# A graph network's edge stage: eight VectorE instructions of 128 elements per step become two of 512

## The reference, cut to what matters

```python
def _layer(x, ea, src, dst, nw, ew, fnw, fnb, few, feb):
    h = relu(x @ nw.T)
    e = relu(ea @ ew.T)
    e2 = concatenate([h[src] + h[dst], e], axis=-1)
    agg = segment_sum(e, dst, num_segments=x.shape[0])
    n2 = concatenate([agg, h], axis=-1)
    n2 = relu(n2 @ fnw.T + fnb)
    e2 = relu(e2 @ few.T + feb)
    return n2, e2
```

## Time and profile before

| | us |
|---|---|
| three runs | 3683.78, 3673.3, 3674.27 |
| median | 3674.27 |
| the profiled execution's own time | 3683.78 |
| its span | 3682.0 |
| busy: TensorE, VectorE, ScalarE, GpSimd | 3343.9, 2011.2, 1169.9, 2618.3 |
| edge-layers stage, first to last gather started | 2552.46 to 3634.35 |
| the last L2305 starts | 3662.0 |
| 200 us of the stage (3000 to 3200), busy: TensorE, VectorE, ScalarE, GpSimd | 187.19, 171.27, 119.34, 153.35 |

### The profile page before, as it was taken

The page is one execution under the profiler, slowest core; times in us unless marked ns, Lnnn a source line. Parts: engine busy times, 40 slices in busy tenths (PEclk is TensorE's granted clock), DMA queues, the critical chain, the costliest instruction groups (busy, mean ns, idle before and its releaser), DMA issues. The chain is left out here.

```text
span 3682.0 us, 74575 instructions
## 1 busy us (share of the span) xinstructions
PE 3343.9 (91%) x22631; PEld 2291.8 (62%) x22631; DVE 2011.2 (55%) x5296; ACT 1169.9 (32%) x2569; POOL 2618.3 (71%) x2750
## 2 busy tenths in 40 slices
PE   2899994999998899999879999986999999999997
PEld 0566662656666565666646566666777777777775
DVE  7675551232324723232661323275788888888887
ACT  1442220000002600000440000055555655556555
POOL 3777776777775677777467777748777777777773
PEclk6899997999999899999989999998999999999998
DMA  7686554777774777777377777746666666666663
GB/s 288 208 262 194 185 183 151 243 237 239 246 241 145 255 243 245 245 244 244 121 263 243 245 243 245 243 133 177 171 166 168 164 165 165 166 167 164 166 166 82
DMA packets 367699, 747.55 MB, mean 203 GB/s; under 512 B 102785, under 2 KB 197659, under 8 KB 366722
## 3 DMA queue, kind: packets, MB, share of 16 engines
q0 software_dynamic: 134912, 331.04, 31.7%
q1 hardware_dynamic: 224679, 362.01, 30.3%
q10 hardware_dynamic: 7899, 51.90, 3.6%
HBM read 613.65 MB, written 131.02 MB: 202 GB/s over the span
## 5 line engine op out<-in xcount | busy, mean ns | idle before, releaser
L601 POOL DMA_INDIRECT ring<-split_table,src_idx x1240 | 1182.1, 953 | 417.3 <-issue 370.8
L1486 PE MATMUL ps<-spare,acc 128*128 128x500 fp8e4 x5292 | 1158.8, 377 | 97.4 <-DMA spare<-adjacency 67.0
L2124 POOL DMA_INDIRECT ring<-h_table,idx_ring x832 | 829.6, 997 | 255.2 <-issue 239.2
L1486 PEld LDWEIGHTS ps<-spare,acc 128*128 128x128 bf16 x5292 | 519.7, 98 | 676.3 <-DMA spare<-adjacency 70.7
L1587 DVE TENSOR_TENSOR onehot<-onehot,ps 128x168 f32<-128x168 f32 x165 | 54.1, 328 | 1029.6 <-PE ps L1497 1006.0
L614 POOL DMA_INDIRECT adjacency<-acc x408 | 411.1, 1008 | 177.2 <-issue 122.3
L1431 ACT ACTIVATE work<-ps 84x256 f32<-84x256 f32 x155 | 58.7, 379 | 1444.1 <-PE ps L1518 1444.1
L1518 PE MATMUL ps<-ring,onehot 128*84 128x256 bf16 x3720 | 432.2, 272 | 2.0 <-DMA ring<-split_table,src_idx 2.0
L1518 PEld LDWEIGHTS ps<-ring,onehot 128*84 128x84 bf16 x3720 | 402.1, 118 | 3.8 <-DMA ring<-split_table,src_idx 2.8
L2134 PE MATMUL ps<-ident,ring 128*128 128x128 f32 x1664 | 258.3, 278 | 70.4 <-DMA ring<-h_table,idx_ring 45.9
L2219 ACT ACTIVATE work<-acc,vecs 128x512 f32<-128x512 f32 x208 | 150.2, 722 | 438.6 <-DVE acc L2278 421.4
(11 more groups left out here) (329 smaller groups left out, 4721.0 us busy)
## 6 DMA issues: line engine op xcount, KB each, us to landing
acc<-split_table SPq DMA_DIRECT2D x104, 768.0 KB, 4.7
spare<-adjacency SPq DMA_DIRECT2D x108, 512.0 KB, 6.3
e_few<-spare SPq DMA_DIRECT2D x104, 512.0 KB, 3.1
acc<-e_few SPq DMA_DIRECT2D x208, 256.0 KB
work<-in_edge_attr SPq DMA_DIRECT2D x104, 256.0 KB
spare<-rel_rows SPq DMA_DIRECT2D x208, 126.0 KB
split_table<-acc ACTq DMA_DIRECT2D x32, 768.0 KB, 3.3
ring<-split_table,src_idx POOLq DMA_INDIRECT x1240
```

What stands on the lines that cost most here:

```text
L601: e.indirect_dma_start(out=to, out_offset=None, in_=table, in_offset=bass.IndirectOffsetOnAxis(ap=src_idx[:, 2 * i + h, j:j + 1], axis=0)) ...
L1486: ins = e.matmul(ps[2 + 2 * c + kind][:, 0:width], split[j % 2][:, k, q, kind * D:(kind + 1) * D], moving, start=(b == q == 0), stop=(b == ...
L2124: e.indirect_dma_start(out=rows[:, s, j, :], out_offset=None, in_=h_table, in_offset=bass.IndirectOffsetOnAxis(ap=idx_ring[:, s, j:j + 1], ...
```

## The change

The two loops over the four rows of edges, which issue one subtraction for each, become one subtraction over all of them. The waits before and the semaphore increments after stay where they are.

```diff
                     if (i - 6).inside(NG):
                         k = i - 6
                         wait(e, S("mid"), k)
-                        for j in range(J):
-                            ins = e.tensor_tensor(parts[k.off % 4][2][:, j, :], left[:, j, :], parts[k.off % 4][1][:, j, :], ALU.subtract)
-                        ins.then_inc(S("low"), 1)
+                        e.tensor_tensor(parts[k.off % 4][2], left, parts[k.off % 4][1], ALU.subtract).then_inc(S("low"), 1)
                     if (i - 5).inside(NG):
                         k = i - 5
                         wait(e, S("high"), k)
                         wait(e, S("low"), k - 1)
-                        for j in range(J):
-                            ins = e.tensor_tensor(left[:, j, :], ring[:, k.off % RING, j, ROW:ROW + D], parts[k.off % 4][0][:, j, :],
-                                                  ALU.subtract)
-                        ins.then_inc(S("left"), 1)
+                        e.tensor_tensor(left, ring[:, k.off % RING, :, ROW:ROW + D], parts[k.off % 4][0],
+                                        ALU.subtract).then_inc(S("left"), 1)
```

## The result

The changed kernel takes 3695.7 us (median of five runs, 3690.9 to 3701.9), the kernel before 3674.3 beside it. The ratio is 1.0053 with a 95% interval of 1.004 to 1.0065: slower by some 20 us, although VectorE has 1248 instructions and 102 us of busy time less. The forecast of 3671 and its range up to 3689 missed it; rival 2 is what happened.

The account below looks back on a forecast made before the run. VectorE with ScalarE was taken to pace the edge-layers stage, GpSimd close behind. About 200 steps x (hold 0.16 to 0.17 - 0.16) - 3 us gave -3 to -1 on 3674.3: forecast 3671, range 3643 to 3689.

Parts of the forecast that it names:

- rival 2: Edge-layers stage: merged instructions hold gathers over 0.23 us per step, making the kernel slower; 3699 us at 0.30; chance 0.23.
- What bounds the kernel: Edge-layers stage: VectorE with ScalarE paces it; GpSimd, free to run at 5.05 us per step, follows at 5.21.
- the circle: Edge-layers stage: VectorE and ScalarE waiting for each other in turn, 5.19 us per step, to shrink by 0.54 to 4.65.
- The rule of the hold: A gather starting under a VectorE instruction with two SBUF inputs is held until its end, then needs 0.83 us.
- The price of an instruction and of the circle: Merged L2305 and L2312 take 0.68 us each; start to start about 0.74; VectorE and ScalarE's turn falls to 4.65.
- How often a gather is held: Edge-layers stage after the change: gathers lose 0.17 us per step in all, about what is lost today.
- settled phase: Edge-layers stage: VectorE follows GpSimd at a steady place, so holds correct themselves; mean loss 0.11 us per step.
- even spread: Edge-layers stage: gathers meet VectorE's long instructions at all places equally; loss 0.235 us per step.
- the lag: Edge-layers stage: from a step's fourth gather's start to TensorE's first transposes 3.38 or 4.38 us, to L2305 6.81 to 7.81.
- the tail: After the last gather the chain lies on VectorE; six L2305 and six L2312 save 3 us.
- the block: Edge-layers stage: L2305 at 0, L2312 at 0.74, L2258 at 1.34, nearly end to end, all over at 2.02 us.
- The end of the run: After the last gather, shorter L2305 and L2312 on VectorE's chain win 3 us for certain.

Follow-up runs that it names:

- g2: Kernel before with the edge-layers stage's gathers replaced by plain DMAs from 128 fixed rows; ratio 0.9198 on a chip where the kernel before took 4483.0 us.
- f1: Kernel before with the one-hot of L2258 made by tensor_scalar instead of tensor_tensor; 3654.9 us against 3679.2, ratio 0.9939.
- f5: Kernel before with each of the two subtractions in two instructions of 256 elements; 3668.9 us, ratio 0.9984.
- g1: Changed kernel with the edge-layers stage's gathers replaced by plain DMAs from 128 fixed rows; 4057.8 us, ratio 0.9034 to the kernel before at 4483.0.
- f2: Kernel before with only the low subtraction merged; 3670.0 us against 3675.8, ratio 0.9978.
- f3: Kernel before with only the left subtraction merged; 3671.8 us against 3675.8, ratio 0.9982.
- f4: Changed kernel with the one-hot of L2258 made by tensor_scalar; 3682.9 us, ratio 1.0018 to the kernel before.
- e1: Kernel before with only the low subtraction merged, on a chip where the kernel before took 4432.5 us; ratio 1.0070.
- e5: Changed kernel with the one-hot of L2258 made by tensor_scalar, on a chip where the kernel before took 4432.5 us; ratio 0.9998.
- e4: Kernel before with the one-hot of L2258 made by tensor_scalar, on a chip where the kernel before took 4432.5 us; ratio 1.0073.

## Why the prediction was wrong

**What bounds the kernel.** Right: VectorE with ScalarE paced the stage, with GpSimd 0.16 us behind its own pace; g2, with no gather held, steps at 5.16, and shortening the circle ends the wait for ScalarE (f1 to f5; 0.5 us of it are left in the changed kernel) and, without indirect gathers, gives 0.34 per step (g1), where TensorE becomes the limit.

**The rule of the hold.** Right in time, to 0.01 us: the holder's end plus 0.83, in the changed kernel too. Summed over its 832 gathers, the rule with tensor_tensor holders alone gives 56 us of hold for the 57 measured. It was too narrow in whom it names: a tensor_scalar with one tensor input holds as well (f1), so two SBUF inputs are enough but not needed. The rule of the Trainium skill that was weighed there (SBUF — State Buffer, section Who interferes with whom) is borne out in its first half: two inputs in SBUF hold, while L2278 and L2283 with a PSUM input don't. The section's inference that tensor_tensor leaves descriptor generation alone fits the plain DMAs of g1 and g2 and is contradicted by the gathers, of which the longest here takes 1.48 us instead of 0.957.

**The price of an instruction and of the circle.** Right: 0.69 and 0.70; L2304 to L2309 takes 0.78 to 0.81 where 0.74 was taken.

**How often a gather is held.** This step failed. It had two numbers, 0.11 for a settled phase and 0.235 for an even spread, and took "the middle of 0.11 and 0.235, 0.17, that is what is lost today". Measured is 57.7 / 208 = 0.277, against 33.4 / 208 = 0.161 before. Two things were wrong in it.

First, the phase doesn't settle. Over 191 steps of each trace I took the place of the first gather that begins after the start of the low subtraction: in the kernel before 168 lie within one eighth of a microsecond, in the changed kernel no such stretch has more than 40, and all places of the 1.26 us between gathers occur. A likely reason is the lag that the prediction had from two steps. From the start of a step's fourth gather to the low subtraction of that step it is 6.45 to 7.40 us in the middle 80% of 180 steps, a spread of nearly 1 us against a spacing of 1.26. The even spread was the case to take, at 200 x (0.235 - 0.16) - 3 = +12; the measured hold of 0.277 gives 208 x 0.117 = +24, and the tail -2.7.

Second, the 0.235 was itself too small, since the block was drawn too tight. In the changed kernel L2309 begins 0.79 and L2258 1.40 us after L2304, where 0.74 and 1.34 were taken, and L1229 reaches 0.08 into L2304. I laid a row of gathers over these places, from every starting place in turn, and applied the rule, with an instruction as holder from 0.03 or from 0.05 us after its start. This estimate gives 0.27 to 0.29 per step, and 0.24 to 0.25 with the places of the prediction. Put down to the instruction under which each gather was held, the holds are 26 us under L2309, 18 under L2304, 10 under L2258 and 3 under L1229 (before, 30 of 33 were under L2258). The prediction's terms give 0.17 / 1.26 x 208 = 28 for L2304 and L2258 together, which is what they measured, 5 for what stands before them, and 17 for L2309: that term was the one mis-sized.

**The end of the run.** Right: -2.7 for the forecast -3.

**The range.** Its upper end, 3689, came from H = 0.25; the price of rival 2, 3699 at H = 0.30, bracketed what came. Its chance of 0.23 was too low because the settled phase, for which only two lags from the stage's first steps spoke, got half the weight.

The same estimate, a free row of gathers over VectorE's instructions as they lie in each trace, comes out at 0.17 to 0.18 for f2 (measured 34.9 / 208 = 0.168), 0.20 for f3 (0.192), 0.21 to 0.22 for f4 (0.212), 0.16 to 0.17 for f5 (0.143) and 0.05 to 0.06 for f1 (0.068, of which 0.012 is the longer undisturbed gather). So an even spread is a fair first price for all the kernels in which GpSimd leads. That it gives 0.17 for the kernel before too, where 0.161 is measured and the phase is locked, is chance.

What stays open: 40 places of 191 in one eighth of a microsecond are twice an even share, so the phase isn't quite even, and what shapes it isn't known. It wasn't tried to fix the phase by a wait. What slows the chips of e1 to e5 and of g1 and g2 stays unknown.

## What to carry to other kernels

Before merging small instructions on one engine, look for another engine that is nearly as full and is stopped by them: shortening the engine that paces is worth at most its distance to the next one (here 0.16 of 0.54 us), while the length of each instruction is what the neighbour waits for. Compare the duration of a gather that begins under each kind of VectorE instruction with its undisturbed one; a value that recurs just above it is a lock of phases, and shows which engine leads. If the leader must be shortened, shorten the instruction that holds longest rather than take away the seams between short ones: f1 does that with L2258, 0.36 us for 0.68, and is 0.6% faster than the kernel before and 1.1% faster than the changed one (0.9939 / 1.0053). And look for the engine behind the next one: here TensorE, at 4.82 us per step, would have ended the gain at 0.34 us even with GpSimd out of the way.

## What the runs showed of the hardware that I had not expected

- A one-hot of 126 x 512 in bf16 takes 0.36 us as tensor_scalar with a per-partition scalar and 0.68 as tensor_tensor with a broadcast input.
- A tensor_scalar with one tensor input holds a gather as a tensor_tensor with two does, until its end plus 0.83 us: 35 cases under L2287 and L2291, and three under the new one-hot (f1, f4, e4).
- It goes both ways. In the changed kernel 27 of the merged subtractions began within 0.04 us of the start of a gather that was not held. They ended 0.72 us after the gather's start, so that they took up to 0.77 us instead of 0.69.
- A plain DMA from GpSimd's queue costs it 0.538 us where the gather costs 0.957, and is not held.
- The kernel before took 3674 to 3679 us in three comparisons, and 4433 and 4483 on two other chips; in the profile of e1 GpSimd's gaps then grow from 255 to 558 us while the undisturbed gather stays at 0.96, and all four engines stand still at the same time for 72.6 of 1200 us.
